# A four-stage graph network on one core: buffer clears issued by POOL, table items spread more thinly over the work beside them, and a reordered end of a scan

## The reference

```python
h = relu(layernorm(x)); x = x + L0(h)   # 3 attention passes x 4 heads over all edges
h = relu(layernorm(x)); x = x + L1(h)   # attention + a state-space scan over nodes
                                        #   sorted by degree + gate + feed-forward
h = relu(layernorm(x)); x = x + L2(h)   # weighted neighbour sum, two 256x256 products
h = relu(layernorm(x)); x = x + L3(h)   # plain neighbour sum, two 256x256 products
# L0: hn = batchnorm(h); ft = hn @ W[l,h]; s = leaky(a1[dst] + a2[src])
#     softmax of s over the edges of a target; sum of ft[src] * alpha; + hn @ res_W[l,h]
# L1: perm = argsort(degree + noise); y = mamba(h[perm]) @ out_proj; y back in node order
```

## Time and profile before

| | |
|---|---|
| median of 3 runs | 7553.96 us (7552.70 to 7565.87) |
| profiled execution | 7538.81 us, span 7537.0 us |
| busy in the span | PE 5291.3, DVE 5347.6, POOL 4329.7, ACT 3290.1 us |
| granted TensorE clock, mean | 0.866 of full speed |

### The profile page before, as it was taken

How to read it: one execution, slowest core, us unless ns; L and a number is a source line. 1 busy time by engine, 2 the same in 40 slices (tenths; PEclk the granted TensorE clock), 3 DMA queues, 4 the chain that set the end, 5 groups by cost and what they waited for, 6 DMA issues and landing times. The chain is left out here.

```text
span 7537.0 us, 93661 instructions
## 1 busy us (share of the span) xinstructions
PE 5291.3 (70%) x19936; PEld 3387.9 (45%) x19936; DVE 5347.6 (71%) x11558; ACT 3290.1 (44%) x11052; POOL 4329.7 (57%) x4197
## 2 busy tenths in 40 slices
PE   4656878888888834647777776687666665666665
PEld 4623444444444423224444443465444444444544
DVE  7667678888888864358999997576666665555554
ACT  1123556666666622669899897454000000000000
POOL 2150066655666436027777777433777775777776
PEclk9978989999999965779999998798787887788787
DMA  6113288888888855248999998523666666666666
GB/s 202 19 63 108 109 287 281 277 281 273 279 275 279 244 201 188 92 163 311 321 326 325 322 323 253 145 88 98 231 230 234 228 233 185 215 222 222 223 219 190
DMA packets 557348, 1651.02 MB, mean 219 GB/s; under 512 B 135727, under 2 KB 249019, under 8 KB 528106
## 3 DMA queue, kind: packets, MB, share of 16 engines
q0 software_dynamic: 230192, 816.00, 35.7%
q1 hardware_dynamic: 291372, 799.55, 29.4%
q10 hardware_dynamic: 35372, 30.97, 1.4%
HBM read 1171.96 MB, written 701.99 MB: 249 GB/s over the span
## 5 line engine op out<-in xcount | busy, mean ns | idle before, releaser
L1270 POOL DMA_INDIRECT rows_e<-hidden,unit_src x1760 | 1676.0, 952 | 589.5 <-issue 510.6
L625 POOL DMA_INDIRECT rows_e<-table,unit_src x928 | 1023.6, 1103 | 845.7 <-PE acc_e L830 460.1
L1007 POOL DMA_INDIRECT rows_e<-table,unit_src x928 | 1072.3, 1156 | 362.4 <-issue 270.5
L819 ACT ACTIVATE rows_e<-rows_e 128x64 f32<-128x64 f32 x4640 | 1118.9, 333 | 1.9
L1379 PE MATMUL acc_e<-rows_e,same 128*128 128x256 f32 x1760 | 622.4, 500 | 457.2 <-DMA rows_e<-hidden,unit_src 433.4
L1091 ACT ACTIVATE rows_e<-rows_e 128x64 f32<-128x64 f32 x3712 | 920.0, 333 | 3.8
L1379 PE MATMUL acc_e<-rows_e,links 128*128 128x256 f32 x1760 | 613.4, 494 | 397.9 <-DMA rows_e<-hidden,unit_src 362.6
L1298 DVE SCALAR_TENSOR_TENSOR sums_e<-sums_e,unit_keep,acc_e 128x256 f32<-128x256 f32 x1024 | 486.4, 475 | 536.2 <-PE acc_e L1379 535.0
L830 PE MATMUL acc_e<-rows_e,unit_w 128*128 128x512 f32 (+1 forms) x1856 | 705.8, 527 | 143.7 <-DVE rows_e L812 101.8
L1423 ACT ACTIVATE turned_f<-turn_f 128x512 f32<-128x512 f32 x98 | 58.5, 597 | 1660.4 <-PE turn_f L1395 1660.4
L1379 PEld LDWEIGHTS acc_e<-rows_e,same 128*128 128x128 f32 x1760 | 418.6, 253 | 621.4 <-DMA rows_e<-hidden,unit_src 488.4
(11 more groups left out here) (517 smaller groups left out, 9720.2 us busy)
## 6 DMA issues: line engine op xcount, KB each, us to landing
staged<-sums_e SPq DMA_DIRECT2D x220, 1024.0 KB, 4.6
bc<-bc_rows SPq DMA_DIRECT2D x228, 896.0 KB
summed<-sums_e SPq DMA_DIRECT2D x464, 390.0 KB
summed<-sums_e SPq DMA_DIRECT2D x464, 130.5 KB
rows_e<-table,unit_src POOLq DMA_INDIRECT x1856, 5.2
hots<-hot_e SPq DMA_DIRECT2D x116, 256.0 KB, 4.9
hots<-unit_w SPq DMA_DIRECT2D x116, 256.0 KB, 4.9
rows_e<-hidden,unit_src POOLq DMA_INDIRECT x1760, 3.2
```

The lines of the kernel that those rows point to most:

```text
L625: pool.indirect_dma_start(self.rows[:, v, e, :], None, table, bass.IndirectOffsetOnAxis(unit_src[:, u, e:e + 1], 0)).then_inc(self.landed[ ...
L819: last = act.activation(r, r, ACT.Copy, scale=self.rows[:, v, e, self.WIDTH + h:self.WIDTH + h + 1])
L1007: pool.indirect_dma_start(self.rows[:, v, e, :], None, self.tab, bass.IndirectOffsetOnAxis(unit_src[:, u, e:e + 1], 0)).then_inc(self.land ...
L1270: pool.indirect_dma_start(self.rows[:, v, :], None, hidden[p], bass.IndirectOffsetOnAxis(index[:, u:u + 1], 0)).then_inc(self.landed[v // ...
```

## The change

It has four parts.

1. The 19 clears of `own_firsts` leave ACT's queue ahead of the first `settle()`. POOL issues them, in the first 19 steps of `clear_sums`, ahead of the 50 clears of `summed`.
2. Five small vectors of layer 1 (`side_vecs`, with `ff1_b` as the former `fb`) get root buffers, 48 bytes a partition. ACT loads them at the start behind layer 0's weights and no longer at the merge. The merge waits for eight loads.
3. The item loop takes two steps of `beside` after five of nine items and one after the other four, for 14 steps in nine items where there were 18. In `rank_nodes` the bf16 tile `zero` is replaced by the fp32 tile `zeros`.
4. At the scan's end SP loads `z_s` before it waits for the `bc` loads. `edges.end` is split: `edges.flush()` (the last slots) is issued after the gating and before the four projections, which now copy into four different buffers.

```diff
-            clears = 0
-            chain.wait(act)
-            for first in own_firsts:
-                wide = first.rearrange("(p r) h -> p (r h)", p=P)
-                for c0 in range(0, wide.shape[1], AW):
-                    c1 = min(c0 + AW, wide.shape[1])
-                    act.dma_start(wide[:, c0:c1], zeros[:, 0:c1 - c0]).then_inc(cleared, 16)
-                    clears += 1
             settle()
+        clears = sum(-(-OWN // P * n // AW) for n in (L * H, H))
...
+        for v, given in ((side_vecs[n], a[f"L1_gnn_{n}"]) for n in sides):
+            act.dma_start(v[:, :], given.rearrange("(c p) -> p c", p=P), allow_slow_non_contiguous=True).then_inc(weights_in, 16)
+            weights += 1
         load_noise(noise)
...
             def clear_sums():
+                for first in own_firsts:
+                    wide = first.rearrange("(p r) h -> p (r h)", p=P)
+                    for c0 in range(0, wide.shape[1], AW):
+                        c1 = min(c0 + AW, wide.shape[1])
+                        yield pool.dma_start(wide[:, c0:c1], zeros[:, 0:c1 - c0]).then_inc(cleared, 16)
                 for t in range(T + 1):
                     yield pool.dma_start(summed[t * P:(t + 1) * P, :], zeros[:, :]).then_inc(emptied, 16)
...
-                for _ in range(2):
+                for _ in range(2 if n % 9 in (0, 2, 4, 6, 8) else 1):
                     next(beside, None)
...
+            sp.wait_ge(s_gated, 4 * NG + 2)
+            sp.dma_start(z_s[:, :], gate_rows[:, 1, NP:NP + TS]).then_inc(s_z, 16)
             for b in range(AHEAD):
                 sp.wait_ge(s_bc[b], 16 * (NG * K // AHEAD + 1))
-            sp.wait_ge(s_gated, 4 * NG + 2)
-            sp.dma_start(z_s[:, :], gate_rows[:, 1, NP:NP + TS]).then_inc(s_z, 16)
             finish_sum(NG * MR, 2 * NG, 1)
             copy_sum(2 * NG)
-            pe.wait_ge(s_gated, 4 * NG + 4)
             for w in range(2):
                 gate(NG, 2 * NG, w, 1)
+            edges.flush()
+            pe.wait_ge(s_gated, 4 * NG + 4)
+            spare = [o_s[:, :, :]] + [v[0:ROW, b, 0:2 * D].rearrange("p (b d) -> p b d", d=D) for v, b in ((inp, 0), (inp, 1), (hs, 0))]
             for w in range(2):
                 for n in range(4):
-                    project(4 * NG + 2 * w, w, n, 0)
+                    e = 4 * NG + 2 * w
+                    project(e, w, n, 0)
                     if n % 2:
-                        evict(4 * NG + 2 * w, n)
-                        keep_rows(NG, 4 * NG + 2 * w, w, n)
+                        kept = spare[2 * w + n // 2]
+                        act.wait_ge(s_o, e + n // 2 + 2)
+                        if kept is spare[0]:
+                            act.wait_ge(s_kept, 16 * (4 * NG + 1))
+                        act.activation(kept, o_ps, ACT.Copy).then_inc(s_turned, 1)
+                        row = NG * TS + w * (4 * ROW) + n // 2 * (2 * ROW)
+                        sp.wait_ge(s_turned, e + n // 2 + 2)
+                        sp.dma_start(sorted_y[row:row + 2 * ROW, :].rearrange("(b p) d -> p b d", p=ROW), kept).then_inc(s_kept, 16)
...
-        for n in sides:
-            vecs[n] = lsb(f"v_{n}", [P, 2])
-            act.dma_start(vecs[n][:, :], a[f"L1_gnn_{n}"].rearrange("(c p) -> p c", p=P), allow_slow_non_contiguous=True
-                          ).then_inc(weights_here, 16)
...
-        fb = lsb("fb", [P, 2 * D // P])
-        act.dma_start(fb[:, :], a["L1_gnn_ff1_b"].rearrange("(c p) -> p c", p=P), allow_slow_non_contiguous=True
-                      ).then_inc(weights_here, 16)
-        all_loaded = 16 * (len(names) + len(sides) + 5)
+        fb = vecs["ff1_b"]
+        all_loaded = 16 * (len(names) + 4)
```

More of the change, by code:

```diff
@@ L408, in rank_nodes @@
                 tri_low = lsb("tri_low", [P, P])
-                one, zero = lsb("one", [P, 1], BF16), lsb("zero", [P, P], BF16)
+                one = lsb("one", [P, 1], BF16)
                 parts = lsb("parts", [P, T, 6])
@@ L414, in rank_nodes @@
                 sp.dma_start(keys[:, :], key_row.partition_broadcast(P)).then_inc(key_in, 16)
-                chain.apart((dve, lambda: dve.memset(one[:, :], 1.0)), (dve, lambda: dve.memset(zero[:, :], 0.0)),
+                chain.apart((dve, lambda: dve.memset(one[:, :], 1.0)),
                             (dve, lambda: dve.memset(parts[:, :, :], 0.0)),
                             (dve, lambda: dve.tensor_scalar(tri_low[:, :], iota[:, :], lane[:, 0:1], None, ALU.is_lt)))
-                chain.step(pe, lambda: pe.matmul(later_ps, zero[:, :], zero[:, 0:T], start=True, stop=False, skip_group_check=True))
+                chain.step(pe, lambda: pe.matmul(later_ps, zeros[:, 0:P], zeros[:, 0:T], start=True, stop=False, skip_group_check=True))
                 chain.wait(dve)
@@ L1177, in begin, with flush @@
                         slot(0, v, "first")
+            def flush(self):
+                for v in range(self.STORE):
+                    for slot in (self.act_slot, self.dve_slot, self.pe_slot, self.sp_slot):
+                        slot(self.ROUNDS, v, "last")
             def end(self, top):
                 n = self.ROUNDS
-                for v in range(self.STORE):
-                    for slot in (self.act_slot, self.dve_slot, self.pe_slot, self.sp_slot):
-                        slot(n, v, "last")
                 dve.wait_ge(self.s_neg, n * self.GROUPS)
@@ L1520, in run @@
                 nc.all_engine_barrier()
+        sides = ("ln_local_g", "ln_local_b", "ln_global_g", "ln_global_b", "ff1_b")
+        side_vecs = {n: sb(f"v_{n}", [P, a[f"L1_gnn_{n}"].shape[0] // P]) for n in sides}
         scored0 = ExitStack()
@@ L2524, in graph_stack_kernel @@
         names = ("gat_b", "ln2_g", "ln2_b", "ff2_b")
[L2525 to L2526 removed]
+        vecs = dict(side_vecs)
         weights_here = sem("weights_here")
```

2 lines of the change are left out of this document (removed).

## The result

The changed kernel takes 7485.57 us in the median of 4 runs (7479.92 to 7490.01), against 7559.91 us (7552.70 to 7566.74, 4 runs) for the kernel before beside it: a ratio of 0.9909, 95% interval 0.9893 to 0.9925. On 7554 us that is 69 us less (57 to 81); 68 were forecast. The two medians lie 74 us apart. The profiled execution took 7479.92 us, its span 7478.0.

A forecast was written before the change was run, and what follows sets the result against it. No single engine bounds the whole, so the sum went place by place: 17 + 42 + 4 + 5 = 68 us off the 7554 us median gives 7486 us, range 7462 to 7516.

The forecast's parts named there:

- Start, 17 us: Kernel start: 16.78 us of ACT's clear issues leave the path ahead of the barrier; gain 17 us, ends 14 and 17.
- Tables, 42 us: Tables and ranks: the 57.9 us tail goes, less 2, 10 and 4 us; gain 42 us, ends 56 and 20.
- 4 more for the last rank steps: End of ranks: the last dozen steps compare few columns, so items there cost an estimated 4 us, hidden by nothing.
- 184 to 215: Rank stretch: PE needs 184 us at 1.72 us an item, 215 at 2.09, both under DVE's 217.
- Scan end, 4 us: Scan's end: early `z_s` and edge sums ahead of the projections start the next stage at 4792; gain 4 us.
- the projections' start: Scan's end: ACT's weightings end at 4766.5 and the last PE sum takes 1.9 us, so projections start at 4768.4.
- three groups at 3.75: Scan's end: three projections stay at 3.75 + 0.69 us and one takes 1.98 + 0.6, ending at 4784.3.
- the other end for fast matmuls: Scan's end: if the fast 1.98 us held for all projections, the gain would be 10 us.
- Merge, 5 us: Merge: without `fb`, DVE's wait ends sooner and the step after next comes at about 4811.5; gain 5 us, ends 2 and 7.
- `f`'s landing: Merge: the last weights `f`, landing at about 4814, were put at 4810 with fewer loads ahead, when DVE is ready.
- The bound behind it: Merge: ten `y_all` gathers from 4793 us on hold the step after next at about 4811.5, where about 4817 was.
- one of my own signs of being wrong: Later, unchanged stretches: the forecast is wrong if one of them moves by more than a few us.

The follow-up runs named there:

- the run with the wait split: Changed kernel, its merge's first layer norm waiting only for the four broadcast vectors, PE waiting for the matrices: 7947.79 us, against 7953.38 for the changed kernel beside it.
- the first group: Runs on the first chip of the kernel before with one of the four parts of the change at a time; the kernel before took 7549.31 us.
- Part 2 alone: Kernel before with only the five side vectors loaded at the start, plus the fp32 zeros tile: 7556.61 us, ratio 1.001 (1.0002 to 1.0019).
- parts 1 and 4 alone: Two runs on the kernel before: only the clears moved to POOL, 7535.55 us; only the scan's end changed, 7539.59 us.
- the second group: Runs on another chip testing shifted addresses, 32 bytes more, edge sums behind the projections, and clears on ACT; the kernel before took 8076.22 us.
- part 1 alone: Kernel before with only the 19 clears moved from ACT's queue to POOL: 7535.55 us, ratio 0.9983 (0.9975 to 0.9992).

## Why the prediction held, point by point

The forecast was 7486 us, and the median 7485.6. That they agree to a microsecond is luck: the interval is 12 us wide either way, the kernel before was 6 us slower beside this run than in the median that the forecast started from, and of the four terms two were off, in opposite directions (+6.8 and -4.1 us). The other two, which make up most of the gain, were right in size.

- **Start, 17 us: right.** 17.5 us in the trace; the run alone gave 13 (6 to 19). POOL issued the moved clears at 0.556 us, forecast from 0.551. The counts grew by 0.8 us. The five small loads stayed hidden in ACT's idle time. With the clears on ACT instead, the start was as early: what cost time was that the issues stood ahead of the barrier.
- **Tables, 42 us: right.** 40.8 in the trace, 42 (32 to 51) alone. From the first item to the end of the ranks it was 511.6 us before and is 521.8, so the slowdown is 10.2, where I had 10 and 4 more for the last rank steps; of the tail 6.83 us stayed, where I had left 2. These two errors offset each other. The 10.2 are DVE's waits, 110.3 us before and 120.5 after, and they do not sit where I looked for them: those for the plan's PE steps (`unit_src`) fell from 12.2 to 7.9 us, but those for `own_ps`, the transposes behind the windows, rose from 5.2 to 13.5, and those for the loads of `begin` ahead of the windows from 29.0 to 37.0, while that for `keys` fell from 6.6 to 0.9. PE's share in the ranks is 195.93 of 227 us, 86%, where I worked out 184 to 215. Tables and ranks end 3 us apart, as the count of steps had it.
- **Scan end, 4 us: mechanism right, size wrong.** 10.8 us in the trace. Of the terms, the projections' start, forecast 18.5 us behind the last scan, came at 17.2. The step that failed is "three groups at 3.75": at 1.89 to 1.98 us they are 5.4 us shorter. I had named 10 us as the other end for fast matmuls, but had not asked what PE does just ahead of them. The runs showed that with the edge sums first the clock is back by the first projection. `z_s` helped less than forecast: it gated 10.1 us after the last scan's start instead of 11.9, while I had 8.5.
- **Merge, 5 us: wrong.** 0.9 in the trace, and the run with the old loads but shifted addresses has 22.4 us, so the edit's own share is about nothing. The step that failed is `f`'s landing. I took 13.6 us from issue and a few less for cleared queues, 17.8 us after the merge's start; the second half of `f` was issued 4 us earlier than before and took 18.3 us, so it landed 22.6 us after the start. In the 14 us ahead of that the core's DMA engines were busy throughout (share 1.03, 344 GB/s; before 1.09 and 335). That the load waited for them fits this and was not tested by itself. The bound behind it I had nearly right: `y_all` at 4811.5, 19.3 us after the start, and the run with the wait split shows 20.2. But even with that bound reached, the first plain gather came no earlier than in other runs, so no run shows that these 5 us could be had.
- **Stretches left alone** moved by +10.2, +5.9 and -11.0 us, more than the "few us" that I allowed, so one of my own signs of being wrong came. Over the single profiled executions of the first group, the close of layer 0 lies between 413.8 and 428.9 us, and the scan rounds between 1337.3 and 1352.3, whatever was edited. One profiled execution can't carry a claim of 5 us there. The +5.9 of the preparation is another matter: it is there in every run of the first two groups with moved addresses, as shown above. They sum to +9.7 us with the other unedited stretches, which is why the profiles differ by 59.5 us and the edited stretches, with the counts, by 69.2.
- **The part that costs.** Part 2 alone was slower by 7 us (1 to 14). In before's order of items, both runs with tiles 160 bytes further have a joint stretch of 569 to 572 us against 562.6 to 564.0 in the five without (before, parts 1 and 4 alone, and two of the second group); nearly all of it arises before the first rank step. With the spread items it is 517.7 to 519.3 against 516.0. The cause was not found; alignment to 64 bytes is excluded, for the changed kernel at least. As the total of the run with addresses alone did not rise, a cost to the whole is not shown.
- **The sum.** Ratios of the four parts alone add up to 0.9928, 54 us, against 0.9909, 69 us, with all. The five intervals together leave some 20 us either way on that difference of 15, so no interplay is shown.

**The rule on POOL's queue.** The trace after has both sides again. This is POOL in the plan stretch of the changed kernel, where DVE compares without a gap and then waits, against the earlier trace rows:

```profile
375.57 19.84 POOL L451 DMA_INDIRECT own_first<-score_at,first_row  x1 [0.30 <-issue]
395.71 17.84 POOL L451 DMA_INDIRECT own_first<-score_at,first_row  x1 [0.30 <-issue]
413.86 0.96 POOL L451 DMA_INDIRECT own_first<-score_at,first_row  x1 [0.30 <-issue]
```

Indirect scatters stall beside DVE's comparisons, and direct clears beside the same kind of comparison issue in 0.556 us. The Trainium skill, "SBUF — State Buffer", section "SBUF: two separate sides", tells of POOL's transfers stalling beside a DVE operation in a two-port mode, and advises issuing from ACT or SP there. The scatters stall as it tells (19.84 and 17.84 us beside the comparisons, 0.96 behind them), though no run shows whether these comparisons are of that mode. The clears do not stall, and its advice did not pay for them: moved to ACT they cost 1.70 and 2.13 us an issue; on the kernel before the ratio was 0.9969 (0.9957 to 0.9981) against 0.9983 (0.9975 to 0.9992) with POOL, which tells no difference, and with the side vectors ahead of them the counts were 10 us longer.

## What to carry to other kernels

When a wait for several loads is cut, work out the landing of every other thing that the same block needs, and take the latest as the bound of the gain: here a wait shorter by 13.6 us brought the next step 4.1 us forward and the total nothing measurable. When matmuls on a chain of latencies sit behind a gap of some microseconds, try other PE work that can bear the low clock ahead of them. And items spread thinly through a serial chain took away three quarters of a tail. The same items put in a block into the chain's longest gap ran out of buffers, whose stores stood in another queue behind the cause of the gap, and then stood in front of what the chain waited for: before filling a gap, check that the filler's own loads, copies and stores can move in it.

## What the runs showed of the hardware

- **Three chips, two speeds.** The same changed kernel took 7486 us on one chip (that of the first group) and 7953 us on another; the kernel before took 7549, 8020 and 8076. The extra lies in the stretches with many transfers, most of it in the plain layers. Here are 2000 us of them, in the changed kernel on the first and then on the third chip:

```profile
5300.00:7300.00 2000.00, 1266.54 (x4162) 929.89 (x4160) 1172.83 (x3715) 99.53 (x227) 1481.79 (x1557) 0.81 0.68 222
```

```profile
5300.00:7300.00 2000.00, 1103.41 (x3531) 777.46 (x3532) 1034.72 (x3279) 94.01 (x220) 1301.31 (x1359) 0.75 0.59 193
```

  POOL issued 1359 gathers instead of 1557, at 0.958 us each instead of 0.952, so it stood more, and 193 GB/s moved instead of 222. The stretches bound by DVE were the same to 1 us (counts 316.4 against 316.1, joint stretch 519.3 against 518.7).
- **The price of issuing one transfer depends on the queue and on what is under way.** The 19 clears cost 0.88 us each on ACT's queue in the start, 0.556 on POOL's, 1.70 on ACT's with POOL's 50 clears under way, and 2.13 with the side vectors' loads ahead of them as well, on another chip. What sets these prices was not tested.
- **The low clock lasts differently long behind the same gap.** In the six profiled executions with the old end of the scan, PE is idle for 6.1 to 6.4 us ahead of the gate, and then three projections run at 3.75 us in three of them (42.2 to 42.4 us for the stretch), two in one (41.0), and one in two (39.6 in both). Timelines of PE, first with part 1 alone, then with part 2 alone:

```profile
4767.84 3.75 PE L2319 MATMUL o_ps_t<-wo,gated 128*112 128x256 f32 x8 [6.33 <-DVE gated L2312]
4772.28 3.75 PE L2319 MATMUL o_ps_t<-wo,gated 128*112 128x256 f32 x8 [0.69 <-ACT o_s L2328]
4776.73 1.98 PE L2319 MATMUL o_ps_t<-wo,gated 128*112 128x256 f32 x8 [0.69 <-ACT o_s L2328]
```

```profile
4794.36 3.73 PE L2326 MATMUL o_ps_t<-wo,gated 128*112 128x256 f32 x8 [6.33 <-DVE gated L2319]
4798.78 1.98 PE L2326 MATMUL o_ps_t<-wo,gated 128*112 128x256 f32 x8 [0.69 <-ACT o_s L2335]
```

  So this stretch of before is worth 42.3 us in the profile that the forecast was made from, and up to 3 less in others; the new order is free of it.
